# Four-block transformer on one core: exponentials for VectorE first, an earlier normalisation, and a second buffer for GpSimd's products

## What is computed

```python
x = x + tanh(g_xattn[0]) * L0_xattn(layernorm(x), ctx, ctx, ...)
x = x + tanh(g_ffn[0])   * L0_ffn(layernorm(x), ...)
x = x + tanh(g_xattn[1]) * L1_xattn(ctx, layernorm(x), mask, ...)
x = x + tanh(g_ffn[1])   * L1_ffn(layernorm(x), ...)      # 8 experts, top 2

# L0_xattn: attention between the 16 heads of ONE token, not between tokens
Q, K, V = (q @ Wq + bq), (k @ Wk + bk), (v @ Wv + bv)      # each (b, s, 16, 16)
score = einsum('bsid,bsjd->bsij', Q, K) / 4                # 16 x 16 per token
w = softmax(score, axis=-1)
attn = einsum('bsij,bsjd->bsid', w, V) @ Wo + bo

# L0_ffn: relu hidden layer of 1024, hidden and w2 rounded to an 8-bit float
out = quantize(quantize(relu(x @ w1.T + b1)) @ quantize(w2).T + quantize(b2))
```

## Time and profile before

| | |
|---|---|
| runs | 2112.92, 2118.34, 2119.60 us, median 2118.34 |
| profiled execution, its own time | 2116.76 us |
| its span | 2115.0 us |
| busy over the span: PE, DVE, ACT, POOL | 90%, 74%, 55%, 44% |
| mean granted TensorE clock | 0.954 of full speed |

### The profile page before, as it was taken

The page is one execution under the profiler, slowest core; times in us unless marked ns, Lnnn a source line. Parts: engine busy times, 40 slices in busy tenths (PEclk is TensorE's granted clock), DMA queues, the critical chain, the costliest instruction groups (busy, mean ns, idle before and its releaser), DMA issues. The chain is left out here.

```text
span 2115.0 us, 36023 instructions
## 1 busy us (share of the span) xinstructions
PE 1902.5 (90%) x11968; PEld 1329.2 (63%) x11968; DVE 1563.4 (74%) x3233; ACT 1156.6 (55%) x2414; POOL 921.6 (44%) x683
## 2 busy tenths in 40 slices
PE   5899999986669999998999999929999999999998
PEld 2566666665223434343434343419999999999998
DVE  7999999993466677776767778547777777777775
ACT  2356665655335555655555655515555666666663
POOL 6999999981633334352434331112222222222222
PEclk8899999998679999999999999959999999999999
DMA  5222222210425151524242441037666666666661
GB/s 172 111 91 111 88 111 111 84 58 1 112 57 123 31 125 60 112 66 105 78 100 91 89 118 34 31 104 254 223 223 217 217 226 228 226 230 226 220 213 60
DMA packets 140067, 271.47 MB, mean 128 GB/s; under 512 B 13915, under 2 KB 91823, under 8 KB 134066
## 3 DMA queue, kind: packets, MB, share of 16 engines
q1 hardware_dynamic: 128812, 244.55, 37.6%
q0 software_dynamic: 10624, 25.26, 3.2%
q10 hardware_dynamic: 518, 0.27, 0.0%
HBM read 201.96 MB, written 71.39 MB: 129 GB/s over the span
## 5 line engine op out<-in xcount | busy, mean ns | idle before, releaser
L1447 DVE CUSTOM_DVE_ANT_0 x_dump<-x_ps,x_bias_q 128x512 bf16<-128x512 f32 x512 | 353.0, 689 | 103.5 <-PE x_ps L1140 90.4
L1316 ACT ACTIVATE x_PT<-x_ps 128x512 f32<-128x512 f32 x512 | 292.2, 601 | 231.5 <-PE x_ps L1155 228.7
L1929 ACT ACTIVATE X<-m_ps 128x256 f32<-128x256 f32 x312 | 119.1, 382 | 226.0 <-PE m_ps L1866 226.0
L1833 POOL DMA_INDIRECT out_dram<-e_y,e_label x78 | 78.9, 1011 | 362.5 <-DVE e_y L1985 350.6
L1140 PE MATMUL x_ps<-x_KS,x_QS 96*128 96x512 bf16 x512 | 200.7, 393 | 26.2 <-DVE x_mx L1447 25.7
L1154 PE MATMUL x_ps<-x_bias_k,x_ident_b 128*128 128x512 bf16 x512 | 196.8, 384 | 2.2 <-issue 1.1
L1155 PE MATMUL x_ps<-x_QS,x_KS 98*128 98x512 bf16 x512 | 196.5, 384 | 0.0
L1968 DVE TENSOR_TENSOR X<-X,m_ps 128x256 f32<-128x256 f32 x312 | 120.5, 416 | 97.0 <-ACT X L1929 92.5
L1866 PE MATMUL m_ps<-e_x_lo,m_hi 128*128 128x256 f32 x640 | 181.3, 283 | 1.5 <-DVE e_x_lo L1953 1.5
L1866 PE MATMUL m_ps<-e_x_hi,m_hi 128*128 128x256 f32 x640 | 180.9, 283 | 0.0
L1866 PE MATMUL m_ps<-e_x_hi,m_lo 128*128 128x256 f32 x640 | 180.7, 282 | 0.0
(11 more groups left out here) (309 smaller groups left out, 5462.9 us busy)
## 6 DMA issues: line engine op xcount, KB each, us to landing
m_raw<-in_L_ffn_w_dram SPq DMA_DIRECT2D x117, 1024.0 KB, 5.2
expert_in<-a_blank SPq DMA_DIRECT2D x34, 1032.0 KB, 4.3
parts<-x_part SPq DMA_DIRECT2D x24, 512.0 KB, 3.8
m_x<-expert_in SPq DMA_DIRECT2D x39, 258.0 KB, 4.8
next_mask_k<-in_maskT_dram SPq DMA_DIRECT2D x32, 256.0 KB, 2.6
next_mask_q<-in_mask_dram SPq DMA_DIRECT2D x29, 256.0 KB, 2.8
x_KS<-parts SPq DMA_DIRECT2D x16, 384.0 KB, 11.0
x_QS<-parts SPq DMA_DIRECT2D x8, 576.0 KB, 6.4
```

The costliest lines, as they stand in the source:

```text
L1316: act.activation(PT[unit % 2][:, k, :], ps_st[e % 3], ACT.Exp, scale=DH ** -0.5).then_inc(exp_done, 1)
L1447: dve.tensor_tensor_reduce(out=dump[:, :], in0=ps_max[m % 2], in1=bias_q[b % 2][:, q, :], scale=1.0, scalar=NEG, op0=ALU.add, op1=ALU.max, ...
L1929: act.activation(silu[f % 2], ps_h[f % 4][:, 0:BLK], ACT.Silu).then_inc(silu_done, 1)
```

## The change

Three edits, all in `first_layer`:

1. `exp(t)` on ScalarE writes the 112 exponentials for VectorE (`ps_e`) first and the 256 for GpSimd (`e_`) behind them. Since the second one is now the later, VectorE waits for `e_ready` ahead of the denominator.
2. `normalise(t + 3)` moves from the end of ScalarE's round to the place behind `exp(t)`.
3. `pool_qk` is there twice. `scores(t)` writes buffer `t % 2` and waits only until `add_scores` two tiles back has been done; `add_scores` reads the same buffer.

```diff
-        pool_qk = sb("pool_qk", [P, (QK_A + QK_B) * H * H])
+        pool_qk = two("pool_qk", [P, (QK_A + QK_B) * H * H])
...
             def scores(t, block):
                 pool.wait_ge(q_copied, t + 1)
-                wait(pool, s_ps, t)
-                pool.tensor_tensor(slices(pool_qk[:, 0:QK_A * H * H], QK_A), queries(...), keys(...), ALU.mult).then_inc(a_made, 1)
+                wait(pool, s_ps, t - 1)
+                products = pool_qk[t % 2]
+                pool.tensor_tensor(slices(products[:, 0:QK_A * H * H], QK_A), queries(...), keys(...), ALU.mult).then_inc(a_made, 1)
...
             def add_scores(t):
...
-                    pe.matmul(ps_s, ident_f[:, :], pool_qk[:, at(d)], start=(d == 0), stop=False)
+                    pe.matmul(ps_s, ident_f[:, :], pool_qk[t % 2][:, at(d)], start=(d == 0), stop=False)
...
             def exp(t):
                 act.wait_ge(s_ready, t + 1)
                 wait(act, pv_made, t - 1)
+                act.activation(ps_e, sm[:, 0:PV_OWN * H], ACT.Exp).then_inc(e_ps, 1)
                 act.activation(e_[t % 2][:, :], sm[:, :], ACT.Exp).then_inc(e_ready, 1)
-                act.activation(ps_e, sm[:, 0:PV_OWN * H], ACT.Exp).then_inc(e_ps, 1)
...
                 if within(t):
                     exp(t)
+                if within(t + 3):
+                    normalise(t + 3)
...
                 if within(t - 1):
                     f_statistics(t - 1)
-                if within(t + 3):
-                    normalise(t + 3)
...
             def own_values(t):
                 dve.wait_ge(e_ps, t + 1)
                 steps.done(dve.tensor_tensor(heads(own_pv[:, :], PV_OWN), ...))
+                dve.wait_ge(e_ready, t + 1)
                 steps.done(dve.tensor_reduce(den[:, :], e_[t % 2][:, :]..., AX.X, ALU.add))
```

More of the change, by code:

```diff
@@ L272, in scores @@
                 pool.wait_ge(q_copied, t + 1)
-                wait(pool, s_ps, t)
-                pool.tensor_tensor(slices(pool_qk[:, 0:QK_A * H * H], QK_A), queries(q_sb[t % 2][:, 0:QK_A * H], QK_A),
+                wait(pool, s_ps, t - 1)
+                products = pool_qk[t % 2]
+                pool.tensor_tensor(slices(products[:, 0:QK_A * H * H], QK_A), queries(q_sb[t % 2][:, 0:QK_A * H], QK_A),
                                    keys(k_sb[t % 2][:, QK_OWN * H:(QK_OWN + QK_A) * H], QK_A), ALU.mult).then_inc(a_made, 1)
-                pool.tensor_tensor(slices(pool_qk[:, QK_A * H * H:], QK_B), queries(q_sb[t % 2][:, QK_A * H:], QK_B),
+                pool.tensor_tensor(slices(products[:, QK_A * H * H:], QK_B), queries(q_sb[t % 2][:, QK_A * H:], QK_B),
                                    keys(k_sb[t % 2][:, (QK_OWN + QK_A) * H:], QK_B), ALU.mult).then_inc(b_made, 1)
@@ L281, in scores @@
                 pool.wait_ge(b_made, t + 1)
-                into = pool_qk[:, (QK_A - FOLD) * H * H:QK_A * H * H]
-                pool.tensor_tensor(into, into, pool_qk[:, QK_A * H * H:(QK_A + FOLD) * H * H], ALU.add).then_inc(folded, 1)
+                into = products[:, (QK_A - FOLD) * H * H:QK_A * H * H]
+                pool.tensor_tensor(into, into, products[:, QK_A * H * H:(QK_A + FOLD) * H * H], ALU.add).then_inc(folded, 1)
             def weighted(t):
@@ L346, in add_scores @@
                 for d in late:
-                    mm = pe.matmul(ps_s, ident_f[:, :], pool_qk[:, at(d)], start=False, stop=(d == late[-1]))
+                    mm = pe.matmul(ps_s, ident_f[:, :], pool_qk[t % 2][:, at(d)], start=False, stop=(d == late[-1]))
                 mm.then_inc(s_ps, 1)
```

## The result

The changed kernel takes 2102.55 us (median of four runs, 2097.15 to 2104.16) against 2118.84 us of the kernel before (median of four, 2112.92 to 2119.60): 16.3 us less, ratio 0.9923 with a 95% interval of 0.9901 to 0.9945. In a second comparison, on another occasion, the ratio was 0.9942 (0.9921 to 0.9962). The forecast was 2104.2 us, 14.1 us less than the median of the three earlier runs of the kernel before (2118.34).

A forecast was written before the change was run, and what follows sets the result against it. A PE/ACT loop was taken to bound the first stage's steady rounds. 11.6 us steady plus 2.5 early, 14.1 off the profiled 2116.8, give 2102.7; the runs' median lies 1.6 higher: 2104.2 us, range 2098 to 2113.

The forecast's parts named there:

- Who sets the pace: First stage's steady rounds: a loop of PE and ACT through `xn` sets the pace, mean 14.18 us; DVE only trails.
- What PE needs: Steady rounds: PE needs 13.02 us short and 13.40 long, below DVE's need by 0.32 and 0.56.
- The size of the waits: DVE's wait for the exponentials falls to 0.33 us each, from 25.5 to about 11 in total; rounds 13.34 and 13.96.
- The steady rounds: 21 first-stage rounds in which DVE's wait falls from 0.88 to 0.33 us, together 11.6 us.
- The early rounds: First-stage rounds gaining 0.31 us each, 8 counted, 2.5 us; gain handed back where DVE waits for the output projection.
- The tail: The last two rounds of the first stage: counted as gaining nothing, since the gain is handed straight back.
- the mark: First stage's end, taken at VectorE's first instruction behind it: some 14 us earlier, from there on the same lengths.
- The second buffer: GpSimd's products in the first stage: its wait for PE goes, one for `e_` comes; worth 0.
- (a): Rival: first stage's relu pays for the moved normalisation in full; 8.3 us steady and 2.5 early saved, 2107.5; chance 0.14.
- (b): Rival: PE's steady round does not shorten, something else being as late as `xn`; only 2.5 us remain, 2115.8; chance 0.11.
- (c): Rival: GpSimd's second buffer is worth its whole gap in the first stage, 29.4 us, 2089; chance 0.02.
- (d): Rival: PE's granted clock falls in the steady rounds, 6.3 us slower, 2124.6 or more; chance 0.06.

The follow-up runs named there:

- e1_swap: The kernel before with only the two exponentials exchanged and the wait ahead of the denominator; 2117.06 us, ratio 0.9990.
- e2_move: The kernel before with only the normalisation moved behind the exponentials; 2113.66 us, ratio 0.9979.
- e7_fill: The whole change plus VectorE's `f_update` moved between the maxima and the product with the probabilities; 2094.10 us, ratio 0.9895 to the kernel before.
- e8_fill_no_buffer: The whole change with VectorE's `f_update` moved ahead of the product with the probabilities, but without the second `pool_qk`; 2095.24 us, ratio 0.9900 to the kernel before.
- e4_buffer: The kernel before with only the second buffer of GpSimd's products (`pool_qk`); 2117.43 us, ratio 0.9994.
- e5_after_again: The whole change unaltered, run once more for its profile; 2103.40 us, ratio 0.9942 to the kernel before.
- e3_no_buffer: The whole change without the second buffer of GpSimd's products (`pool_qk`); 2106.31 us, ratio 0.9930 to the kernel before.
- e6_twice: The whole change with a second, unused normalisation pass of the same size after `normalise`, from tile 4 on; 2103.26 us, ratio 0.9931 to the kernel before.

## Why the prediction was right

- **Who sets the pace.** The loop of PE and ACT through `xn` was read from two waits of about 1 us of PE and from who was late for whom. e1_swap confirms it in the hardest way, by gaining nothing in the steady rounds, and e2_move by gaining the 0.24 of lateness and no more.
- **What PE needs.** The prediction had it 0.15 us too long, 13.02 and 13.40, and so the slack too small, 0.32 and 0.56. Measured are waits for `on` of 0.47 and 0.70, and in e7_fill rounds of 13.02 and 13.62 in which PE still waits 0.15 and 0.38: its need is 12.87 and 13.24. The noted wait of 0.93 for `xn` was not all that the round lost. From the last sums of the round to the turning of `xn` it is 218.97 - 215.72 = 3.25 us before and 227.65 - 225.49 = 2.16 after, 1.09 less. The lines of before, then of after:

```profile
215.72 2.32 PE L347 MATMUL a_ps<-a_pool_qk,ident_f 128*128 128x256 f32 x10
```

```profile
225.49 2.32 PE L348 MATMUL a_ps<-a_pool_qk,ident_f 128*128 128x256 f32 x10
...
227.65 0.38 PE L308 MATMUL a_ps<-ident_f,a_xn 128*128 128x128 f32 x2
```

The turning starts 2.16 us after the first of these matmuls, although the group is noted with 2.32. The error fell on the safe side, as VectorE sets the pace.

- **The size of the waits.** Forecast 0.33 at L583, measured 0.33 to 0.34 in 30 of 32 rounds and 0.44 in two; total forecast about 11 us, measured 10.9. The rounds of 13.34 and 13.96 came out at 13.35 and 13.95.
- **The steady rounds.** Forecast 11.6 us for 21 of them, measured 10.84 in 20 and 0.60 in the next: 11.4.
- **The early rounds.** Forecast 2.5 us, measured 1.98 at tile 9. The term was somewhat too large, and two profiles cannot size it well: where the rounds at a low clock fell moved tile 9 by 2.3 us between e7_fill and e8_fill_no_buffer (last section), and e4_buffer reached it 0.5 later than the kernel before. Where VectorE waits for the output projection, the gain is handed back, as forecast; the wait grew from 0.70 to 1.01, though in a round one earlier (timeline of the kernel after), and to 0.91 in e5_after_again, so that the match with 0.31 is chance:

```profile
112.67 0.48 DVE L605 SCALAR_TENSOR_TENSOR X<-a_ps,tanh_g,X 128x256 f32<-128x256 f32 x1 [1.01 <-PE a_ps L336]
```

- **The tail** gave about 1 us that the sum did not have, 14.47 - 11.44 - 1.98; its rounds vary with the granted clock (above). That the mark moved by 14.47 for 14.1 is luck to this extent: the steady and the early rounds gave 0.7 us less than forecast, and the tail 1.05 more.
- **The second buffer** at zero: e4_buffer and e3_no_buffer for the steady rounds; e8_fill_no_buffer shows a worth in the tail once the rounds are shorter still. The sentence of the Trainium skill's page "Perfetto Trace Analysis", section Optimization Strategy, on the same gap repeating holds with its own condition, "on the engine that should be saturated": GpSimd's gap was as regular as can be, 1.33 and 0.91 us by turns, and removing its cause moved it by one instruction, to the product ahead of the one that had waited.
- **The rivals.** (a) The relu did not pay: it started 1.97 us after PE's turning of `on` in the kernel after (220.05 - 218.08), as in the kernel before (210.66 - 208.70 = 1.96), and e6_twice shows that when a second insertion does delay it, PE's slack takes the delay in. The prediction had up to 0.1 sticking out. (b) and (c) are refuted by the 20 rounds and by e4_buffer. (d) The clock stayed at 1.00 in the steady part, with waits for `on` of 0.47 and 0.70 us in its rounds, and in e2_move with 0.8 to 1.0. The first relu of the kernel before:

```profile
210.66 0.84 ACT L485 ACTIVATE a_hq<-a_ps,a_b1c 128x256 fp8e4<-128x256 f32 x2 [0.64 <-PE a_ps L358]
```

- What the measured total has beyond the sum, 16.3 us for 14.1, lies within the spread of the runs (2097.15 to 2104.16). The profile of the kernel after is of the fastest of its four executions; its 19.6 us should not be explained by the change.

## What to carry to other kernels

When an engine waits a little in every round, ask who is late for whom before pricing the wait: here VectorE's wait of 0.88 us was 0.33 of latency, 0.31 of order and 0.24 of another loop's lateness, and the two edits were worth 0.0 and 4.7 us apart and 10.7 together. A regular gap on an engine that nobody waits for moved when its cause was removed, and cost nothing; once the others' rounds are shorter, look again whether somebody waits. Once an engine's round is its own instructions and one short latency, put something of its own that depends on nothing recent into that latency (6 us here for moving one line).

## What the runs showed of the hardware

The stages behind the mark took between 1580.6 and 1592.7 us in ten profiles whose later stages hold the same instructions. Part of the spread can be placed: from the mark to the first matmul of the expert stage it is 1424.58 - 529.25 = 895.3 us before, 1404.09 - 514.78 = 889.3 after and 1430.13 - 528.15 = 902.0 in e1_swap, while from there to the end of the span it is 690.4, 691.3 and 690.7. Over all ten profiles the first part takes 889.3 to 902.0 us and the second 690.2 to 691.4. So the spread is in the second attention stage. It goes with TensorE's granted clock there: a mean of 0.94 in the 889.3 us, 0.93 in the 895.3 and 0.92 in the 902.0. The whole times do the same: of the twelve executions of the kernel before beside e5 to e7, those with a mean clock of 0.956 to 0.958 took 2112.56 to 2116.10 us, and those with 0.951 to 0.955 took 2117.26 to 2124.84. What moves the clock from one execution to the next was not tried. The two profiles of the whole change differ by 8.3 us, 0.4%, in their spans, so a comparison of two single spans says nothing below that, while the 20 rounds of the first stage repeat to 0.03 us in 273.

The granted clock of the early rounds and of the tail also differed between profiles of equal code: between 124 and 138 us it was 0.89 before, and 1.00 in both profiles after, with a low one a round or two earlier in its place. Such a round costs about 1.1 us: from tile 4 to tile 5 the clock was 0.88 in e7_fill and 1.00 in e8_fill_no_buffer, and VectorE's round took 14.13 and 13.03 us; from tile 6 to tile 7 it was 0.90 and 1.00, and 14.08 and 13.01. These two rounds are the 2.3 us between the two kernels at tile 9. What decides the moment was not settled.
